# A two-layer graph network on one core: stage two's intermediate rows in PSUM, the sums copy moved, 38 chunks of x kept in SBUF

## The reference, cut to what matters

```python
h = jnp.maximum(_layernorm(x, axis=-1), 0.0)
x = x + _L0_gnn_ref(h, edge_index, ...)      # layer 0
h = jnp.maximum(_layernorm(x, axis=-1), 0.0)
x = x + _L1_gnn_ref(h, ...)                  # layer 1

# layer 0
gate = silu(edge_attr @ W1.T + b1) @ W2.T + b2 + adapt_logit
msg = gate * h[dst] * (cw * mj)[:, None]
agg = segment_sum(msg, src) / clip(segment_sum(mj, src), 1e-08)[:, None]
x = h + agg
return (x - mu) / jnp.sqrt(var + LN_EPS) * gamma + beta

# layer 1
h1 = relu(einsum('ni,rij->nrj', inputs, weight1) + bias1)
h2 = einsum('nrj,rjo->nro', h1, weight2)
agg = segment_sum(h2[src, rel_type] * norm, dst)
return relu(agg + bias2)
```

## Time and profile before

| what | us |
|---|---|
| median of 3 runs (1553.53 to 1558.82) | 1557.85 |
| the profiled execution | 1553.13 |
| its span, first to last instruction | 1551.4 |
| VectorE busy | 1328.8 (86%) |
| TensorE busy | 1134.8 (73%) |
| GpSimd busy | 1060.9 (68%) |
| ScalarE busy | 611.9 (39%) |

### The profile page before, as it was taken

The page is one execution under the profiler, slowest core; times in us unless marked ns, Lnnn a source line. Parts: engine busy times, 40 slices in busy tenths (PEclk is TensorE's granted clock), DMA queues, the critical chain, the costliest instruction groups (busy, mean ns, idle before and its releaser), DMA issues.

```text
span 1551.4 us, 20014 instructions
## 1 busy us (share of the span) xinstructions
PE 1134.8 (73%) x5198; PEld 841.7 (54%) x5198; DVE 1328.8 (86%) x3937; ACT 611.9 (39%) x1423; POOL 1060.9 (68%) x809
## 2 busy tenths in 40 slices
PE   5899998999989989870078777777888777775000
PEld 3677776777777777760045555545555555553000
DVE  6999999999999999960699899999999999983589
ACT  2545445444444454430144444444444444442000
POOL 7655567787887776666468888888888888875000
PEclk9655566555665565555556666666666666667555
DMA  7999986666666666632556666555556555533899
GB/s 237 318 320 311 326 220 152 152 145 158 143 158 137 144 164 140 151 62 11 187 158 168 159 165 151 138 130 125 129 137 138 137 137 133 135 70 57 328 389 391
DMA packets 155542, 271.86 MB, mean 175 GB/s; under 512 B 73947, under 2 KB 90540, under 8 KB 154533
## 3 DMA queue, kind: packets, MB, share of 16 engines
q1 hardware_dynamic: 79380, 226.68, 43.8%
q0 software_dynamic: 68992, 24.64, 18.4%
q10 hardware_dynamic: 7056, 19.27, 3.1%
HBM read 195.91 MB, written 114.13 MB: 200 GB/s over the span
## 4 chain that ended last, share of the span: by engine, by line
POOL 25%; PE 25%; DVE 20%; DMA 14%; issue 12%; ACT 3%; SPq 1%; POOLq 0%; ACTq 0%; DVEq 0%
PE ps_s L551 12%; POOL agg L500 10%; POOL agg L464 9%; POOL t L491 5%; DMA agg<-sums,once 3%; PE ps_k L625 2%; DMA agg<-u,once 2%; PE ps_s L589 2%; DVE ynrm L1014 2%; DVE ygam L1016 2%; PE ps_q L581 2%; DMA kept_in<-x_mid 2%; PE ps_k L538 2%; DVE t L807 2%; PE ps_k L539 2%
## 5 line engine op out<-in xcount | busy, mean ns | idle before, releaser
L551 PEld LDWEIGHTS ps_s<-msg,same 128*128 128x128 f32 x1960 | 386.3, 303 | 31.2 <-issue 29.1
L551 PE MATMUL ps_s<-msg,same 128*128 128x49 f32 (+1 forms) x1960 | 391.1, 382 | 3.0 <-DVE msg L918 2.0
L500 POOL DMA_INDIRECT agg<-sums,once x196 | 325.4, 1660 | 77.6 <-issue 57.6
L491 POOL DMA_INDIRECT t<-agg,src_all x196 | 217.6, 1110 | 81.6 <-issue 51.2
L422 POOL DMA_INDIRECT nodes<-in_table,dst_all x196 | 195.7, 999 | 103.4 <-issue 50.1
L625 PE MATMUL ps_k<-h_t,rw_sb 56*128 56x256 f32 x588 | 118.9, 519 | 138.1 <-ACT hid L717 136.4
L625 PEld LDWEIGHTS ps_k<-h_t,rw_sb 56*128 56x128 f32 x588 | 62.5, 241 | 176.5 <-ACT hid L717 157.0
L638 PE MATMUL ps_m<-hid,rw_sb 128*64 128x256 f32 x588 | 135.4, 631 | 0.0
L538 PE MATMUL ps_k<-types_lo,low_hot 128*128 128x392 bf16 x196 | 95.5, 487 | 45.3 <-DVE low_hot L801 44.2
L807 DVE SCALAR_TENSOR_TENSOR t<-iota_hi,hi_all,ps_k 128x392 f32<-128x392 f32 x196 | 113.7, 616 | 1.8 <-PE ps_k L539 1.8
L530 PEld LDWEIGHTS ps_k<-centre,xt 96*128 96x128 f32 x392 | 70.3, 269 | 61.7 <-issue 61.7
(11 more groups left out here) (150 smaller groups left out, 2521.5 us busy)
## 6 DMA issues: line engine op xcount, KB each, us to landing
agg<-in_both SPq DMA_DIRECT2D x14, 2758.0 KB, 13.3
t<-agg SPq DMA_DIRECT2D x49, 784.0 KB, 4.7
kept<-kept_out SPq DMA_DIRECT2D x49, 404.0 KB
kept_in<-kept SPq DMA_DIRECT2D x49, 404.0 KB, 5.4
agg<-bias_rows SPq DMA_DIRECT2D x49, 384.0 KB, 4.3
out<-t ACTq DMA_DIRECT2D x49, 384.0 KB, 5.9
rows<-in_src_rows SPq DMA_DIRECT2D x49, 256.0 KB, 4.1
rows<-in_dst_rows SPq DMA_DIRECT2D x49, 256.0 KB, 3.4
```

The source lines that it names most:

```text
L491: pool.indirect_dma_start(t2[b % T2S][:, t, :], None, wide, bass.IndirectOffsetOnAxis(ap=src_all[:, c:c + 1], axis=0)).then_inc(ends_in[b ...
L500: pool.indirect_dma_start(agg1, bass.IndirectOffsetOnAxis(ap=once1[b % LAG1][:, t:t + 1], axis=0), sums1[b % LAG1][:, t, :], None, compute ...
L551: last = mm(ps_s[:, t * width:(t + 1) * width], kept_same[:, at:at + P], m[:, v, :], start=(v == t), stop=(v == TILES - 1))
```

## The change

Six things change.

- `u`, `ynrm` and `ygam` no longer exist in SBUF. One tile `v` of 20 x 48 in PSUM takes all three in turn; ygam is written over ynrm in place. `ktot` and `yrstd` are columns behind it. The three take 1000 of the 1024 columns of two PSUM banks, which are ps_q and ps_s in stage one. A wait for the x2 of the block before stands ahead of u.
- To free these banks, the transposes of msg1_t go to the second half of ps_t, whose first half takes the transposes of h2, and the sums of duplicates go to the second half of ps_m, whose first half takes the product with the second weights.
- The waits that this needs: TensorE's h2 transposes await the reading of the former msg1, its sums await msg1_t's copy (m1_copied), and ScalarE's copy h_t awaits the transposes of msg1_t (m1t_done).
- ScalarE's copy of the sums moves from before the square roots to behind them and behind the wait for m1_done.
- The ring of sums in stage one, and agg_last and x_last in stage three, lie in other tiles (y, ysq, x2, hid1, t2).
- RES is 38: four more chunks of x stay in SBUF, and 11 instead of 15 go through x_mid.

The diff, without context lines:

```diff
--- before.py
+++ after.py
@@ -62 +62 @@
-RES = 34
+RES = 38
@@ -127,2 +126,0 @@
-        ktot = sb("ktot", [P, G])
-        u = sb("u", [P, G, H])
@@ -134,3 +131,0 @@
-        yrstd = sb("yrstd", [P, G])
-        ynrm = sb("ynrm", [P, G, H])
-        ygam = sb("ygam", [P, G, H])
@@ -156,2 +150,0 @@
-        sums = [v[:, :, :].rearrange("p r h -> p (r h)")[:, k * TILES * AW:(k + 1) * TILES * AW].rearrange("p (t w) -> p t w", w=AW)
-                for v in (u, y, ysq, ynrm, ygam) for k in range(4)][0:LAG]
@@ -230,2 +223,8 @@
-        agg_last = [v[:, 0:NR, :].rearrange("p r h -> p (r h)") for v in (u, y, ysq, ynrm)]
-        x_last = [v[:, 0:PC] for v in (kept_in[0], kept_in[1], kept_in[2], ygam[:, :, :].rearrange("p r h -> p (r h)"))]
+        halves = hid1[:, :, :, :].rearrange("p k h n -> p (k h n)")
+        agg_last = [y[:, 0:NR, :].rearrange("p r h -> p (r h)"), ysq[:, 0:NR, :].rearrange("p r h -> p (r h)"),
+                    halves[:, 0:PC], halves[:, PC:2 * PC]]
+        x_last = [w[:, 0:PC] for w in (kept_in[0], kept_in[1], kept_in[2], t2[2][:, :, :].rearrange("p r w -> p (r w)"))]
+        sums_in = ([(w[:, :, :].rearrange("p r h -> p (r h)"), 4) for w in (y, ysq, x2[0], x2[1])]
+                   + [(hid1[:, :, :, :].rearrange("p k h n -> p (k h n)"), 7)])
+        sums = [w[:, k * TILES * AW:(k + 1) * TILES * AW].rearrange("p (t w) -> p t w", w=AW)
+                for w, fit in sums_in for k in range(fit)][0:LAG]
@@ -239 +237,0 @@
-        ps_q = psum("ps_q", [P, 512])
@@ -241 +239,7 @@
-        ps_s = psum("ps_s", [P, 512])
+        ps_qs = psum("ps_qs", [P, 2, 512])
+        ps_q, ps_s = ps_qs[:, 0, :], ps_qs[:, 1, :]
+        ps_flat = ps_qs[:, :, :].rearrange("p a n -> p (a n)")
+        v = ps_flat[:, 0:G * H].rearrange("p (r h) -> p r h", h=H)
+        ktot = ps_flat[:, G * H:G * H + G]
+        yrstd = ps_flat[:, G * H + G:G * H + 2 * G]
+        ps_sums1 = ps_m[:, BE // 2:BE // 2 + TILES * H]
@@ -547 +551 @@
-            def sums_within(width, kept_same, m):
+            def sums_within(ps, width, kept_same, m):
@@ -551 +555 @@
-                        last = mm(ps_s[:, t * width:(t + 1) * width], kept_same[:, at:at + P], m[:, v, :],
+                        last = mm(ps[:, t * width:(t + 1) * width], kept_same[:, at:at + P], m[:, v, :],
@@ -561 +565 @@
-                sums_within(AW, same[b % 2], msg[b % 2]).then_inc(S["sums_done"], 1)
+                sums_within(ps_s, AW, same[b % 2], msg[b % 2]).then_inc(S["sums_done"], 1)
@@ -601,0 +606 @@
+                    need(pe, S["msg1_done"], f)
@@ -613 +618 @@
-                        last = nc.tensor.transpose(ps_q[:, t * P:(t + 1) * P], msg1_t[:, t * P:(t + 1) * P], ident[:, :])
+                        last = nc.tensor.transpose(ps_t[:, BE // 2 + t * P:BE // 2 + (t + 1) * P], msg1_t[:, t * P:(t + 1) * P], ident[:, :])
@@ -632 +637,2 @@
-                    sums_within(H, same[f % 2], msg1).then_inc(S["sums1_done"], 1)
+                    pe.wait_ge(S["m1_copied"], f + 1)
+                    sums_within(ps_sums1, H, same[f % 2], msg1).then_inc(S["sums1_done"], 1)
@@ -697,0 +704 @@
+                    need(act, S["m1t_done"], g + 1)
@@ -706 +713 @@
-                        last = A(msg1[:, t, :], ps_q[:, t * HALF:t * HALF + H], ACT.Copy, scale=norm_all[:, c:c + 1])
+                        last = A(msg1[:, t, :], ps_t[:, BE // 2 + t * HALF:BE // 2 + t * HALF + H], ACT.Copy, scale=norm_all[:, c:c + 1])
@@ -731,4 +737,0 @@
-                if 0 <= g:
-                    act.wait_ge(S["sums1_done"], g + 1)
-                    need(act, S["added1"], 16 * TILES * (g - LAG1 + 1))
-                    nc.scalar.copy(sums1[g % LAG1][:, :, :].rearrange("p t w -> p (t w)"), ps_s[:, 0:TILES * H]).then_inc(S["sums1_copied"], 1)
@@ -750,0 +754,5 @@
+                if 0 <= g:
+                    act.wait_ge(S["sums1_done"], g + 1)
+                    need(act, S["added1"], 16 * TILES * (g - LAG1 + 1))
+                    nc.scalar.copy(sums1[g % LAG1][:, :, :].rearrange("p t w -> p (t w)"), ps_sums1).then_inc(S["sums1_copied"], 1)
+                if 0 <= f < NBLOCK:
@@ -946 +954 @@
-                    V.tensor_tensor(ktot[:, :], rtot[:, :], kin[:, ST:ST + G], ALU.mult).then_inc(S["ktot_done"], 1)
+                    V.tensor_tensor(ktot, rtot[:, :], kin[:, ST:ST + G], ALU.mult).then_inc(S["ktot_done"], 1)
@@ -954 +962,2 @@
-                    V.tensor_tensor(u[:, :, :], on[:, :, AW:AW + H], cols(ktot[:, :], H), ALU.mult).then_inc(S["u_done"], 1)
+                    need(dve, S["x2_done"], b)
+                    V.tensor_tensor(v, on[:, :, AW:AW + H], cols(ktot, H), ALU.mult).then_inc(S["u_done"], 1)
@@ -967 +976 @@
-                    V.tensor_tensor(y[:, :, :], u[:, :, :], kin[:, 0:S2 + PC].rearrange("p (r f) -> p r f", f=H), ALU.add).then_inc(S["y_done"], 1)
+                    V.tensor_tensor(y[:, :, :], v, kin[:, 0:S2 + PC].rearrange("p (r f) -> p r f", f=H), ALU.add).then_inc(S["y_done"], 1)
@@ -1012 +1021 @@
-                    V.reciprocal(yrstd[:, :], ystd[:, :]).then_inc(S["yrstd_done"], 1)
+                    V.reciprocal(yrstd, ystd[:, :]).then_inc(S["yrstd_done"], 1)
@@ -1014 +1023 @@
-                    V.tensor_tensor(ynrm[:, :, :], y[:, :, :], cols(yrstd[:, :], H), ALU.mult).then_inc(S["ynrm_done"], 1)
+                    V.tensor_tensor(v, y[:, :, :], cols(yrstd, H), ALU.mult).then_inc(S["ynrm_done"], 1)
@@ -1016 +1025 @@
-                    V.tensor_tensor(ygam[:, :, :], ynrm[:, :, :], each(gamma_b[:, :], G), ALU.mult).then_inc(S["ygam_done"], 1)
+                    V.tensor_tensor(v, v, each(gamma_b[:, :], G), ALU.mult).then_inc(S["ygam_done"], 1)
@@ -1020 +1029 @@
-                    V.tensor_tensor(x_rows(b), ygam[:, :, :], on[:, :, 0:H], ALU.add).then_inc(S["x2_done"], 1)
+                    V.tensor_tensor(x_rows(b), v, on[:, :, 0:H], ALU.add).then_inc(S["x2_done"], 1)
```

## The result

The changed kernel takes 1535.4 us (median of 4 runs, 1529.3 to 1539.0) against 1558.3 of before on the same chip: ratio 0.984, 95% interval 0.981 to 0.988. The forecast was 1523.6, its range 1511 to 1547. The profiled execution took 1533.91 us, its span is 1532.2.

What follows compares the result with a forecast made beforehand. In stage two VectorE (by a wait) and GpSimd (by holds) were each kept at 13.43 us a period. Steady part -31.1, ends +1.0, stage three -4.1: -34.2 us, from the median 1557.85 to 1523.6; range 1511 to 1547.

Steps and rivals of the forecast that it cites:

- rival A: VectorE's PSUM writes cost latency, seven instructions 0.56 us more, so VectorE binds at 13.1 us; time 1536, chance 0.16.
- Both cures: Stage two: VectorE's 0.89 us wait and GpSimd's holds must both go; with one alone the period stays 13.43 us.
- The copy moved: ScalarE's later sums1 copy removes VectorE's 0.89 us wait before erstd; its lateness adds 0.04 us to GpSimd's period.
- GpSimd's own 12.76: GpSimd's stage-two period once the long gather's 0.67 us hold goes, with the third add's 0.18 from cen kept.
- Rival E: The hold by cen goes too and the copy is in time: GpSimd at 12.58 us, time 1516, chance 0.04.
- The cover of the moved copy: ScalarE's work queued behind the copy ends near 1110.2, before asq at 1110.9: 0.7 us left, so no cost.
- Operands in PSUM: With one operand in PSUM, u, y, ynrm, ygam and x stop holding GpSimd; the long gather's 0.67 us goes.
- Rival C: The gather meeting ynrm is held whatever its operands; GpSimd stays at 13.43 us, time 1554, chance 0.08.
- PSUM's price, nought: VectorE's instructions reading or writing PSUM take no longer; the Trainium skill's rule would give an estimated 0.46 us.
- D: VectorE writes PSUM in two passes, three instructions 1.0 us more each; VectorE 15.54 us, time some 1639, chance 0.07.
- Rival B: GpSimd's fourth add is held by a comparison, up to 0.5 us; period 13.26, time 1543, chance 0.13.
- The start: Stage two's first adds await the copy, 2.8 us later in its loop: + 1 us, of bounds 0 and 2.8.

Runs made afterwards that it cites:

- the kernels at 15.15 and 14.27: The changed kernel with u, ynrm, ygam, ktot, yrstd in SBUF and 34 chunks: 1630.0 us; the same with gathers one block further ahead: 1593.6 us.
- With the loop cut: The changed kernel with gathers one block further ahead (AHEAD1 7 for 6): 1526.8 us; with VectorE's tot in PSUM as well: 1540.2 us.
- two pairs of kernels: The changed kernel without and with AHEAD1 = 7 (1535.4, 1526.8 us); the same two with tot in PSUM (1534.2, 1540.2 us).

## Why the prediction was right, point by point

The part that was right is that GpSimd's holds are what the change takes away, that PSUM costs VectorE nothing, and that four chunks save 4 us. The profiled execution was forecast at 1518.9 us and took 1533.9, 15.0 more. By the table above: 5.9 lie ahead of stage two, 1.0 in its start, 7.2 in its periods, 1.1 in its end, and -0.2 in stage three. The median lies 11.8 above the forecast and within its range. But the prediction also named a sign by which it would be wrong, a period outside 12.6 to 12.9 us, and the period is 12.94: by its own sign it missed, if by little. In time alone rival A's 1536 is the nearest, by chance, since its cause isn't there.

- **"Both cures".** The reading of one period was right, the conclusion not. "Each is kept at 13.43" held only as long as the two engines met as they did there. The wait lifted alone made 14.20 (slower, not the same). The operands moved with VectorE's wait nearly restored made 13.14, with VectorE at the pace of its wait, as the step says, but on the mean 0.4 below before (not none). The step took the holds as a sum belonging to GpSimd, while they depend on which instruction meets which.
- **The copy moved, "I add 0.04".** This term was mis-sized, in the place for which the prediction named the sign (a wait of GpSimd for the copy). The copy itself was about as early as forecast, 11.12 us from asum's start to its end (forecast 1108.00 - 1096.95 = 11.05). But the step let the add start at the copy's end, and the rows show 0.77 us between. Half of 12.73 + 12.41 would be 12.57 a period; with half of 0.77 it is 12.96. GpSimd's idle time grew by 0.12 a period in place of 0.04.
- **GpSimd's own 12.76 came out by luck.** Its instructions and their gaps make 12.8. But the 0.18 that was left in it for cen isn't there: cen now ends (1105.57 + 0.35 = 1105.92) before the third add begins (1106.35). (Rival E had named this half, with the copy in time, which it wasn't.) In its place the fourth adds are held, 1.71 in the mean against 1.54, and some second adds, as the one at 1104.33 (1.71) that starts while ac has 0.26 us to go. The period would come out the same with other holds only by accident: without any it is 12.61.
- **The cover of the moved copy** held: h_t's copy and the msg copies end at 1102.95 + 0.88 = 1103.83, and asq starts at 1104.62.
- **Operands in PSUM.** All four gathers are unheld beside ynrm and ygam. With the rows in SBUF again they are back, in the kernels at 15.15 and 14.27. Rival C, the hold not lifted, falls.
- **PSUM's price, nought,** was right. u 1153 ns (1151 before), ynrm 1161 (1160), ygam in place 1166 (1160), y 1150 (1152), x 1157 (1158), yrstd 278 (270), ktot 175 (166). Rivals A and D fall. The rule of the Trainium skill, Perfetto Trace Analysis, section Optimizing Scalar/DVE Operations, from which the prediction estimated 0.46 us a round, is not borne out: the seven differences add up to less than 0.03 us. The rule of the Trainium skill, SBUF — State Buffer, section Who interferes with whom, that a VectorE instruction with a single SBUF input doesn't contend with GpSimd, is: none of the instructions with one operand in PSUM held a gather in the steady part.
- **Rival B**, the fourth add held by a comparison, is there in small: 24 of 41 fourth adds take 1.77 to 1.92, such as the one at 1120.87, against the 1.54 of 1108.20. The comparison of 384 columns (0.61 long) began at 1120.64: 1.54 + (1121.25 - 1120.87) - 0.12 = 1.80. With the loop cut this hold decides between 12.61 and 12.93 (medians).
- **The start**, +2.0 against +1.0, lies inside its bounds. **The end**, +1.1 against nought, stays unexplained.
- **Stage three**, -4.3 against -4.1, was right.
- **Ahead of stage two** I forecast no change, and the pair has +5.9. Over the profiled executions of kernels whose stage one is the same but for where its sums lie, the first gather is anywhere from 736.1 to 758.1 us, with the changed kernel at 743.9 and at 752.0. A difference of 5.9 is within the spread of executions, so nothing here makes it a term of the change.

Left open: how much of the gain the operands bring by themselves with the copy in its old place. Two banks are needed for them, the copy's own would have to go, and so no such kernel was tried. Nor was it tried to keep the fourth add free of the comparisons in the changed kernel with the loop left as it is, so what the loop costs by itself is known only from two pairs of kernels: 0.26 us a period where the hold went too, 0.07 where it stayed.

## What to carry to other kernels

When two engines hold each other up, a wait that one of them has may be what keeps them apart; count what the freed engine will meet before counting its wait as a gain. For a loop over several engines, add the time from an instruction's end to the start of the one it releases, read at a place where the release comes last, because the trace may show it as "issue" and not as a wait. If such a loop binds, one more block of lead (here one constant) opens it, but what that gives depends on the next bound, which may be close: here 0.07 or 0.26 us a period. To see which, split an engine's period into the lengths of its instructions and its idle time, since a held instruction shows as a long one and not as a wait.
